# All 64 tiles in straight line in place of a loop on every engine, in a cross-attention and FP4 feed-forward kernel

## What is computed

```
x = x + norm(mlstm(layernorm(x), ctx, ctx, gates)) * norm_w     # 8 heads of 64, causal, decay D
x = x + fp4_linear(silu(fp4_linear(x', w_gate)) * fp4_linear(x', w_up), w_down)    # x' = layernorm(x)
# fp4_linear quantizes both operands in blocks of 16 to the grid 0, .5, 1, 1.5, 2, 3, 4, 6; 512 -> 1408 -> 512
```

## Time and profile before

| | |
|---|---|
| median of 3 runs | 1975.62 us (1973.06 to 1977.54) |
| the profiled execution's own time | 1977.65 us |
| its span, first to last instruction | 1975.9 us |
| TensorE matmuls | 1829.6 us busy, 93% of the span, 12001 instructions |
| VectorE | 1455.9 us, 74% |
| ScalarE | 1452.2 us, 73% |
| GpSimd | 1167.6 us, 59% |
| granted TensorE clock, mean | 0.971 of full speed |

### The profile page before, as it was taken

The page is one execution under the profiler, slowest core; times in us unless marked ns, Lnnn a source line. Parts: engine busy times, 40 slices in busy tenths (PEclk is TensorE's granted clock), DMA queues, the critical chain, the costliest instruction groups (busy, mean ns, idle before and its releaser), DMA issues. The chain is left out here.

```text
span 1975.9 us, 41157 instructions
## 1 busy us (share of the span) xinstructions
PE 1829.6 (93%) x12001; PEld 1031.1 (52%) x12001; DVE 1455.9 (74%) x3213; ACT 1452.2 (73%) x2990; POOL 1167.6 (59%) x1189
## 2 busy tenths in 40 slices
PE   2448999999999999999999999999999999999997
PEld 1334555555555555554555555555555555555553
DVE  8788777777777677776777777777777777778784
ACT  5767687787877777786777777777777877776663
POOL 7675655656565656655565655656566555655652
PEclk9758999999999999999999999999999999999999
DMA  6844444444344434444354443444344444444423
GB/s 198 177 107 103 99 117 110 115 111 115 102 116 110 118 102 116 100 114 106 101 120 106 116 102 101 116 110 118 98 111 109 107 115 113 109 102 94 103 64 71
DMA packets 366406, 218.40 MB, mean 111 GB/s; under 512 B 299168, under 2 KB 305824, under 8 KB 366144
## 3 DMA queue, kind: packets, MB, share of 16 engines
q1 hardware_dynamic: 366144, 215.40, 43.9%
HBM read 126.45 MB, written 17.30 MB: 73 GB/s over the span
## 5 line engine op out<-in xcount | busy, mean ns | idle before, releaser
L1041 POOL TENSOR_TENSOR stage<-stage,hs 128x512 f32<-128x512 f32 (+1 forms) x192 | 224.3, 1168 | 437.5 <-DVE stage L1249 433.3
L482 PE MATMUL bank<-wgTh,xqT 128*128 128x512 f16 (+1 forms) x768 | 281.2, 366 | 27.1 <-DMA xqT<-xqs 23.3
L483 PE MATMUL bank<-wuTh,xqT 128*128 128x512 f16 (+1 forms) x768 | 280.0, 365 | 0.0
L484 PE MATMUL bank<-wgTl,xqT 128*128 128x512 f16 (+1 forms) x768 | 279.7, 364 | 0.0
L487 PE MATMUL bank<-wuTh,xqT 128*128 128x512 f16 (+1 forms) x768 | 279.7, 364 | 0.0
L485 PE MATMUL bank<-wuTl,xqT 128*128 128x512 f16 (+1 forms) x768 | 279.5, 364 | 0.0
L486 PE MATMUL bank<-wgTh,xqT 128*128 128x512 f16 (+1 forms) x768 | 279.3, 364 | 0.0
L597 PE MATMUL bank<-wdTh,work 128*128 128x512 f16 x704 | 268.8, 382 | 11.0 <-DMA work<-stage 11.0
L598 PE MATMUL bank<-wdTl,work 128*128 128x512 f16 x704 | 267.6, 380 | 0.0
L599 PE MATMUL bank<-wdTh,work 128*128 128x512 f16 x704 | 267.5, 380 | 0.0
L1303 DVE TENSOR_TENSOR stage<-stage 128x512 f16<-128x512 f32 (+1 forms) x192 | 156.9, 817 | 102.5 <-ACT stage L723 102.4
(11 more groups left out here) (191 smaller groups left out, 4252.2 us busy)
## 6 DMA issues: line engine op xcount, KB each, us to landing
mb<-max_dram SPq DMA_DIRECT2D x64, 512.0 KB, 3.9
xb<-in_x_dram SPq DMA_DIRECT2D x64, 256.0 KB, 2.8
cf<-in_ctx_dram SPq DMA_DIRECT2D x64, 256.0 KB, 2.7
cn<-in_ctx_dram SPq DMA_DIRECT2D x64, 256.0 KB, 3.0
x<-in_x_dram SPq DMA_DIRECT2D x64, 256.0 KB, 3.1
wb<-warp_dram SPq DMA_DIRECT2D x128, 128.0 KB, 2.9
out_dram<-ob SPq DMA_DIRECT2D x64, 256.0 KB, 3.1
work<-stage SPq DMA_TRANSPOSE x192, 3.1
```

What stands on the lines that cost most here:

```text
L482: e.matmul(g[:, 0:w], hi, wgT[0][:, c, n0:n0 + w], start=first, stop=False)
L483: e.matmul(y[:, 0:w], hi, wuT[0][:, c, n0:n0 + w], start=first, stop=False)
L484: e.matmul(g[:, 0:w], hi, wgT[1][:, c, n0:n0 + w], start=False, stop=False)
L1041: e.tensor_tensor(blocks(hx[:, n0:n0 + w]), blocks(hx[:, n0:n0 + w]), per_block(hs2[:, n0 // BLOCK:(n0 + w) // BLOCK]), ALU.mult).then_inc ...
```

## The change

The loop is taken out. `turns` calls each turn function for `u` = 10 to 74 with a plain number, so all waits compare with constants and all addresses are constants. `Tile` loses its loop index. The order of the operations on every engine stays. With it go three small things: SyncE and GpSimd no longer add to the semaphore `go`; `pe_qk` of tile 0 has two more waits; `pe_u` is written as twelve parts that are issued in the same order.

```diff
 class Tile:
-    def __init__(self, first, j=None):
-        self.first, self.j = first, j
+    def __init__(self, first):
+        self.first = first
...
-    def _plus(self, value, per_loop):
-        return value if self.j is None else self.j * per_loop + value
...
     def done(self, back=0, k=1):
-        return self._plus(k * (self.first - back + 1), 8 * k)
+        return k * (self.first - back + 1)
...
-        LOOP0, LOOPS = 19, 5
...
         def turns(e, turn):
-            for u in range(FIRST, LOOP0):
-                turn(e, u, None)
-            with e.Fori(0, LOOPS) as j:
-                for i in range(8):
-                    turn(e, LOOP0 + i, j)
-            for u in range(LOOP0 + 8 * LOOPS, LAST):
-                turn(e, u, None)
+            for u in range(FIRST, LAST):
+                turn(e, u)
...
-        def sp_wait(e, s, value):
-            e.wait_ge(s, value)
-            e.sem_inc(S_["go"], 1)
-
         def sp_stored(e, t):
-            sp_wait(e, S_["out"], t.done())
+            e.wait_ge(S_["out"], t.done())
...
         def pe_qk(e, t):
             e.wait_ge(S_["xT"], t.done())
             e.wait_ge(S_["cT"], t.done())
+            if t.at_start(0):
+                e.wait_ge(S_["xT"], T[4].done())
+                e.wait_ge(S_["cT"], T[4].done())
...
         def pool_mask(e, t, par):
             e.wait_ge(S_["D"], t.done())
-            e.sem_inc(S_["go"], 1)
```

More of the change, by code:

```diff
@@ L37, in live @@
     def live(self, total):
[L38 removed]
+        return 0 <= self.first < total
     def at_start(self, n):
[L41 removed]
+        return self.first == n
     def has(self, back):
[L44 removed]
+        return self.first >= back
     def back(self, d):
[L47 to L50 removed]
+        return Tile(self.first - d)
     def done(self, back=0, k=1):
[L54 removed]
+        return k * (self.first - back + 1)
     def of(self, k, i):
[L58 removed]
+        return k * self.first + i + 1
     def dma(self, ring, back=0):
[L62 removed]
+        return 16 * ((self.first - back) // ring + 1)
     def quads(self, back=0):
[L66 removed]
+        return (self.first - back) // 4 + 1
     def quads_of(self, k, i, back=0):
[L70 to L76, removed]
+        return k * ((self.first - back) // 4) + i + 1
 def mlstm_fp4_ffn(nc, x, ctx_in, ig_w, ig_b, fg_w, fg_b, norm_w, w_gate, w_up, w_down, out):
@@ L348, in sp_rows_out @@
             if t.slot % 4 == 3:
-                sp_wait(e, S_["gate"], t.quads_of(3, 2))
-                four = bass.ds(t.done(3) - 1, 4)
+                e.wait_ge(S_["gate"], t.quads_of(3, 2))
+                four = slice(t.first - 3, t.first + 1)
                 e.dma_start(max_dram[four, :].rearrange("n (h s) -> (n h) s", h=NH), mw[:, 0, :]).then_inc(S_["max_out"], 16)
-                sp_wait(e, S_["warp"], t.quads())
+                e.wait_ge(S_["warp"], t.quads())
                 e.dma_start(warp_dram[four, :].rearrange("n (h s) -> (n h) s", h=NH), mw[:, 1, :]).then_inc(S_["warp_out"], 16)
@@ L551, in pe_pick_mm, with pe_u_part @@
                 i.then_inc(S_["pick_mm"], 1)
-        def pe_u(e, t):
[L554 to L572, removed]
+        def pe_u_part(e, t, k):
+            later = t.back(-5)
+            if k == 0:
+                if later.live(NT):
+                    e.wait_ge(S_["xT"], later.done())
+                    e.wait_ge(S_["gpart"], later.done())
+                    if later.slot % 4 == 3:
+                        e.wait_ge(S_["gr"], later.quads_of(4, 3))
+                e.wait_ge(s_Sbd[0], t.done())
+                e.wait_ge(s_Sbd[1], t.done())
+                e.wait_ge(S_["xw"], t.done())
+                e.wait_ge(S_["vc"], t.done())
+                e.wait_ge(s_C[0], t.done())
+                e.wait_ge(s_C[1], t.done())
+            c, j = divmod(k, 3)
+            o = U[c // 2][:, c % 2]
+            if j == 0:
+                return e.matmul(o.rearrange("p r d -> p (r d)"), xw[:, c, :], Sbd[:, c, :, :].rearrange("p r d -> p (r d)"),
+                                start=(c % 2 == 0), stop=False)
+            i = e.matmul(o[:, j - 1, :], D[:, j - 1, c, :], vc[t.parity][:, 2 * c + j - 1, :], start=False, stop=(c % 2 == 1 and j == 2))
+            return i.then_inc(S_["u"], 1) if k == 11 else i
+        def pe_u(e, t):
+            for k in range(12):
+                pe_u_part(e, t, k)
         def pe_st_mm(e, t):
```

118 lines of the change are left out of this document (59 added, 59 removed).

## The result

| | before | changed | ratio, 95% interval |
|---|---|---|---|
| the comparison | 1974.97 us (1971.83 to 1978.3, 9 runs) | 1957.44 us (1953.31 to 1967.15, 9 runs) | 0.9915 [0.9897, 0.9933] |
| the same pair again, e5 | 1971.17 us (10 runs) | 1950.73 us (4 runs) | 0.9904 [0.988, 0.9928] |
| once more, e10 | 1970.78 us (9 runs) | 1952.16 us (5 runs) | 0.9905 [0.9888, 0.9922] |

The change gains 17.5, 20.4 and 18.6 us, where 31.7 were forecast. The direction was right. The time is that of the first rival, 1957 us, which had a chance of 0.09.

The account below looks back on a forecast made before the run. TensorE was taken as the bound, slowed in the loop by late hand-overs at turn ends. Loop 1148.15 less 5 x 223.29 gives 31.7; 1975.62 - 31.7 = 1943.9 us, range 1938 to 1950 (0.78), 8 in 10 for 1937 to 1958.

Parts of the forecast that it names:

- first rival: Middle turns: TensorE's code fetches keep colliding with the `xqT` issue, every second turn pays 0.66 us, 13 us; 1957 us, chance 0.09.
- The bound and the place: TensorE bounds the kernel; the hand-over from `dve_x_lo` through the `xqT` DMA to `pe_gu` decides, with 0.4 us margin.
- (a): Loop's four jumps back: 10.9 us in their turns plus 5.1 us of lowered clock behind three, 16.0 us removed.
- (b): Looped turns: register work lets `nr` lose to GpSimd's `un`, 1.17 for 0.17 us, 15 of 40; 15.7 us with (c).
- (c): Every second looped turn: `xqT` transpose issue takes 2.65 us instead of 1.24; 15.7 us removed together with (b).
- slower: All 40 turns: fetch and transpose meet, landing up to 5.7 us, 1.24 us a turn, 49.6 us; 1992 us, chance 0.03.
- the forecast's sum: Loop of 1148.15 us less five written-out octets of 223.29 us: 31.7 us gained, 32.9 without a hiccup.
- The range: Whole kernel, 8 in 10: 1937 to 1958 us, taking in the first rival, the start's gain and half of 4.5 us.
- Increments of `go`: On SyncE and GpSimd: hidden in full turns, so removing them was taken as 0 us.
- the start might gain up to 1.3 us: Kernel's start, where SyncE issues more: gain from the missing `go` increments bounded by 0 and 1.3 us, taken as 0.

Follow-up runs that it names:

- e5: The changed kernel itself, nothing edited, run again in another group of runs: 1950.73 us, ratio 0.9904 to the kernel before.
- e10: The changed kernel, nothing edited, third look, on the same chip as e9: 1952.16 us, ratio 0.9905 to the kernel before.
- e4: The kernel before with 16 turns in the loop's body and 2 passes, the last 8 looped turns written out: 1956.58 us, ratio 0.9935.
- e7: The kernel before, loop kept, with e1's waits left out and 98 idle TensorE instructions in the turn before the loop: 1976.78 us, ratio 1.0033.
- e6: e1 with four idle instructions on VectorE ahead of `nr` in tiles 6 to 57: 1949.18 us, ratio 0.9891.
- e9: The kernel of e1 again, on the same chip as e10: 1940.19 us, ratio 0.9839 to the kernel before.
- e2: e1 with 45 idle instructions ahead of TensorE's first operation: 1961.76 us, ratio 0.9961 to the kernel before.
- e1: The changed kernel with eight already-met TensorE waits left out in tiles 12 to 57, 1536 instructions per four turns: 1940.98 us, ratio 0.9857.
- e3: The changed kernel with the increments of `go` put back on SyncE and GpSimd: 1950.65 us, ratio 0.991 to the kernel before.
- e8: e1 with 128 idle instructions at the head of TensorE's stream: 1948.28 us, ratio 0.989 to the kernel before.

## Why the forecast was half right

**The bound and the place: right.** Nearly all that the change moved is in the middle, at the hand-over from `dve_x_lo` to `pe_gu`. Between the two traces the start, the first octet and the end stayed within 2 us.

**(a) The jumps: right for the traced execution, wrong in one reading.** Forecast 16.0 us. In the changed kernel's trace the four turns are within 0.01 us of clean and the clock holds, so the 10.9 and the 5.1 us are both gone. That each execution of the kernel before pays the 5.1 us isn't shown: the clock fell behind three of the nine jumps in the traces (before, e4, e7). But I had written that at 921.53 us the DMA "had landed by about 918.7", and took it out of the account. It hadn't. I had worked that out from the median flight instead of asking for this one. The line of this very transpose, in the kernel before:

```profile
L345 SPq DMA_TRANSPOSE xqT<-xqs x1: 1243/1243/1243, 915.3 to 915.3; - x1
...
DMA to landing us min/median/max: 5.7/5.7/5.7
```

It landed at 921.0, half a microsecond before TensorE began. So the profile's "2.80 <-DMA xqT" was right for most of the gap. It wasn't right for the end: at every other late opening of this trace TensorE starts 0.05 us behind the landing, at the four jumps 0.6 us behind. For that last part the rows of "issue" stand. The other transfers issued with it were late too, though the traffic of the core didn't stop. Two issues of 915.3 to 921.6 us, with their time to landing, and the traffic of 918 to 921:

```profile
x<-in_x_dram SPq DMA_DIRECT2D x1, 256.0 KB, 4.7
out_dram<-ob SPq DMA_DIRECT2D x1, 256.0 KB, 4.7
...
DMA packets 319, 0.54 MB, mean 180 GB/s; under 512 B 67, under 2 KB 67, under 8 KB 316
```

This did no harm to the sum, as the gap went with the jump, but it hid that transfers land late beside a fetch of code, which is the very thing that was left over.

**(b) The race: right in its mechanism, small in its price.** Not one of the 40 turns of the middle loses it now (15 before). In the changed kernel, all 40 `nr` of the middle, and one pair:

```profile
L1415 DVE SCALAR_TENSOR_TENSOR nr<-uc,cols x40: 167/168/170, 482.9 to 1579.2; 128x8 f32<-128x8 f32 x40
```

```profile
482.89 0.17 DVE L1415 SCALAR_TENSOR_TENSOR nr<-uc,cols 128x8 f32<-128x8 f32 x1 [0.40 <-ACT uc L864]
...
482.93 1.18 POOL L1092 TENSOR_TENSOR un<-uc,nw 128x512 f32<-128x512 f32 x1 [0.45 <-ACT uc L864]
```

But at e6's 0.15 us a turn, 15 turns make 2.3 us. In the loop the price may be higher: in e7's middle the six turns with a lost race and neither a jump nor a fetch beside them are 0.33 us over clean on average, the 25 with none of the three 0.09. In before's trace the two kinds don't differ (0.26 and 0.28 us), so something else of the loop costs as much there, and which part of it isn't shown. I never gave (b) a term of its own; it stood in one sum with (c), 15.7 us.

**(c) The long issue: this is the step that failed.** I took it for one of three costs of the loop, that the change would remove, and so put it at nothing in the changed kernel. There it is 9.3 of the 9.7 us by which the traced middle is over clean, and 12.0 us by the medians of e9 and e10. The forecast's own sign for this, turns over 28 us with long issues, came true. It is no cost of the loop. It is where a packet of TensorE's code falls, and straight-line code has as many packets (12 per octet by rows 10, 61 in 40 turns now). The issue's length wasn't even the harm: in e2's middle all issues take 1.24 us and the landings are late. In the written-out octet before the loop the packets lay in the clear part, and I used its rate, 5 x 223.29, as the rate of forty turns. With 16 instructions of drift in four turns the place moves by 160 in forty turns, more than half a packet, so no octet could stand for all of them. I had even written the drift down, in the first rival, and set against it one turn, tile 51's, that had been covered by the margin. One turn was too little: the margin (0.4 us) covers a landing after 3.8 us, not one after 4.8 as in the turn of rows 11 or after 5.5 as in the changed kernel. The 5.7 us of rows 6, which the rival "slower" took for the worst collision, was the landing at a jump.

**The first rival: right in mechanism, and in size by the medians.** It said 13 us for collisions left over. The same-chip pair e9 and e10 gives 12.0 us between the kernel with its packets held clear and the changed one; the three traces of the changed kernel show 9.3, 8.5 and 6.6 us of them in the middle. Its own working, though, was every second turn at 0.66 us; in truth it is bursts of turns at 0.3 to 2.0 us. The size was met in part by luck.

**The closing sum.** From before to clear (e9, e1): 0.9839 and 0.9857 are 31.7 and 28.2 us; the forecast's sum was 31.7. Of the 32.9 us over clean in the trace of before, the jumps with the clock behind them are 16.0, the collisions 10.2, and the race and what else the loop adds 6.7. In the changed kernel's trace 9.3 us of collisions are left and little else. So the change took the jumps and the 6.7 us, and left collisions that cost about as much as they had cost the loop (9.3, 8.5 and 6.6 us in its three traces). By this the gain would be 23 us; the medians give 17.5 to 20.4. The traced executions of the changed kernel are all under their medians (by 4.1, 1.7 and 3.3 us), and what the others lose no trace shows. More collisions in them, or fewer falls of the clock in before, would both fit.

**The range.** Its lower end, 1937 us, doesn't follow from the terms that are named for it: 1943.9 - 1.3 - 2.25 is 1940.3. The result doesn't turn on it.

**`go`, and the two rules.** Increments of `go` at 0 us: right, by e3. The Trainium skill ("Advanced Engine Details and Errata", Control Flow Timing), by which a branch that compares costs about 0.1 us, doesn't give the price of a jump in these loops: the turns that end in one are 1.7 to 3.0 us long over clean. A second page fits better. The Trainium skill ("Runtime: NRT & Kernel Launch", Instruction fetch mechanics) says that code is refilled in blocks of 16 KiB, 256 instructions, and that a taken branch breaks the prefetch. The trace agrees for TensorE (97 packets for about 24,870 instructions). It also says that the cost of crossing a block is "mostly hidden". Here 60 crossings in the middle cost nothing in e9, and in e2 they cost 12.4 us more than in e1; it depends on what is in flight.

**Start and end.** I had thought that the start might gain up to 1.3 us; it varies by 4 us from execution to execution, so nothing can be said.

## What to carry to other kernels

Writing a loop out takes away its jumps, here 2.4 to 3.0 us of TensorE's time each with eight turns in the body, and some 1.7 us more where the clock falls behind one; a longer body (e4) has fewer of them. It doesn't take away the fetches of code. If a transfer with little slack closes each turn, count the instructions of the tightest engine per period: a multiple of 256 keeps the fetches in one place, for better or worse, and then look whether that place is clear. Before one stretch of a kernel is used as the measure for another, ask what in it has a longer period than the stretch.

## What the runs showed of the hardware that I had not expected

- A 16 KB fetch of TensorE's code can hold up the core's other DMA traffic: in e2 for 1.6 us with at most 11 GB/s, and `x`, `ob` and `xqT` in flight at the time landed after 4.8, 4.8 and 5.4 us, where e1 has 3.2, 3.2 and 3.5.
- It isn't each fetch. In e2's turns that end at tiles 12, 16, 20, 40, 44 and 48 a packet lies beside the hand-over as well. Counted from the issue, it starts 0.2 to 0.6 us later than in most turns of the long kind, takes 1.6 to 1.9 us itself instead of 0.93, and the turn is clean (32 and 36 are exceptions, with 1.1 us and a long turn). Who comes first on the shared path seems to decide; that is an inference from the order in the trace, no run was made for it.
- 45 idle instructions, run once, cost 12.4 us over forty turns by where they put the others (e2 against e1); 128 of them cost nothing there (e8).
- Idle instructions in TensorE's stream amid full turns aren't free: 98 in e7 left it idle for 6.6 us (0.07 us each) and, with the clock at half behind both gaps, cost 11.4 us.
- The clock fell behind jumps with gaps of 2.80, 2.79 and 2.39 us (before) and not behind gaps of 2.25 (before), 2.39 (e4), 2.06, 2.60, 1.51 and 2.02 us (e7). The length of the gap alone doesn't decide it.
- A 128x8 operation of VectorE takes 0.17 us when it starts ahead of GpSimd's 128x512 operation, and 0.93 us when it starts 0.28 us after it, ending as that one ends (e6).
